# Local attention and the last tanh stage with one-pass products of split operands

## The chip, the cores and the metric

The kernel runs on one core of a Trainium2 chip. The metric is the device time of one execution in microseconds (us), the median of several runs. The core's engines are called by their short names: PE (TensorE, matrix products; PEld is its weight loading), DVE (VectorE), ACT (ScalarE), POOL (GpSimd) and SP, which issues DMAs. Each engine works through its own instructions in the order written, and waits on semaphores for the others.

## The reference

Eight sublayers follow each other on an input of 8 x 1024 x 256. Each adds its result to x. The two that the change touches are the first and the last:

```python
x = x + local_attention(layernorm(x), Wq, bq, Wk, bk, Wv, bv)   # the first
# q, k, v = xh @ W.T + b in groups of 64 tokens (1024 / 16 heads along the length)
# out = softmax(q @ k.T) @ v inside each group
...
x = x + tanh(((layernorm(x) @ weight) @ aux1) @ aux2 + bias)    # the last, and one more before
```

Everything is fp32. The other sublayers (two expert layers, a spectral attention, a second-order attention, the other tanh layer, a window attention) are as before.

## The kernel before, in words

x lies in on-chip memory (`R.X`) as 64 tiles of 128 tokens by 256 values. The stages run one after another, with a barrier between them.

**Local attention** (`local_attention`, tiles named `la_...`). Its loop runs over the 64 tiles, and on every engine an iteration i serves several tiles at different steps. The steps of one tile are:

- POOL: `normalize` (L2790) makes the normalised tile `xn`.
- PE: `turn_x` (L2574) transposes it in two pieces of 128 columns. ACT: `copy_xT` (L2654) copies the result to `xnT`.
- PE: `project` makes z = G x (L2585; G is the product of Wq and Wk, folded once at the start) and v (L2591; 273 columns, of which some are not v itself: one is a term that the scores need, eight feed the next stage's gate).
- DVE: `copy_z` (L2718) and `copy_v` (L2727) bring them from PSUM to SBUF. POOL: `add_row` makes `mask_row` (L2797) and `before` (L2798) from v.
- PE: `scores` (L2599). DVE: `mask_S` (L2735) adds `mask_row` and takes the maximum; it waits for `mask_ready`, that is, for the tile's `add_row`. ACT: `exponent` (L2660).
- PE: `turn_p` (L2606), ACT: `copy_pT` (L2667), PE: `weigh` (L2612; it waits for `x_ready` of the tile before).
- DVE: `residual` (L2740, L2744, L2746: reciprocal, gate part, X) and `next_stats` (L2751), the statistics for the next stage. In the first iterations DVE also takes the statistics of the tiles to come (L2687), 24 in iterations 0 to 4 and 32 in iterations 8 to 28.

The order on each engine is written by hand, in the loops at the end of each engine's block. The projection's results, the scores, the transposed probabilities and the output have one PSUM bank each, so the next tile's product waits until DVE or ACT has emptied it.

**Last tanh stage** (`tanh_ffn` with `out` given, tiles `t_...`). The three weights are folded into one matrix `wc` in an earlier stage. For each tile: PE transposes X (L196) four tiles ahead, ACT copies (L221), PE multiplies by `wc` (L204, two products of 256 columns), DVE scales and adds the bias (L246), ACT takes tanh (L227), POOL adds to X (L264), and SP sends eight tiles at a time to the output.

An fp32 product is two instructions on PE in the trace, each with its weight load. The type fp32r is taken in one instruction, with less precision. The expert stages before and after the change already use it: each operand is split into a high part (a copy to fp32r) and a low part (operand minus high), and the product is the sum of high x high, high x low and low x high.

The code with its line numbers:

## Time and profile before

| | |
|---|---|
| median of 3 runs | 3776.21 us (3773.47 to 3776.36) |
| profiled execution | 3772.48 us, of which span 3770.5 |
| PE busy | 3479.7 us, 92% |
| PEld busy | 3107.1 us, 82% |
| DVE busy | 2376.8 us, 63% |
| ACT busy | 2133.8 us, 57% |
| POOL busy | 1515.2 us, 40% |
| local attention | up to 232.9 us from the start, its loop from about 25 |
| last tanh stage | from 3690.5 to the end |

Busy shares are means over stages with different limits. The stage that the change touches most takes 5 to 6% of the span, so what happens there is read from its own stretch: a timeline of one tile, the waits of each engine, and the distance between two instructions of one kind. A line number names the line of the kernel that issued the instruction.

### The profile page before, as it was taken

Reading aid. Unit: us, or ns where it says so; the run is one execution under the profiler, and the core shown is the slowest. Engines: PE = TensorE matmul, PEld = TensorE weight load, DVE = VectorE, ACT = ScalarE, POOL = GpSimd, SP = SyncE. Lnnn points to the kernel's source line nnn. Section 1 sums busy time; section 2 is a strip of 40 time slices with the busy share of each in tenths; the row PEclk is TensorE's granted clock in tenths of the full one; section 3 lists DMA queues with packets and bytes.
Section 4 is the critical chain, followed back from the end, with each engine's and each line's share of the span. In section 5 each row is a group of like instructions: output and inputs, shape, how many; then the busy total and the mean of one; then the engine's idle time right before and its main releaser. Section 6 shows DMA issues by size and latency. Waiting matters only on the chain. (4 is left out here: it accounts for less than half of the span.)

```text
span 3770.5 us, 116189 instructions
## 1 busy us (share of the span) xinstructions
PE 3479.7 (92%) x44738; PEld 3107.1 (82%) x44738; DVE 2376.8 (63%) x6505; ACT 2133.8 (57%) x6562; POOL 1515.2 (40%) x2283
## 2 busy tenths in 40 slices
PE   8948999799849999799999999999988999999998
PEld 7838999677729999799898999989976877777777
DVE  6774555688765554455544444444446899999994
ACT  3345555455446555344444444444444888888895
POOL 3444665210035665344444444444446222222215
PEclk9979999899969999899999999999999999999999
DMA  3143443511153443300000000000000000000002
GB/s 123 39 144 99 93 92 60 146 47 52 50 186 92 93 93 71 101 3 3 3 3 3 3 3 3 3 3 3 3 6 16 2 2 2 2 2 2 2 2 94
DMA packets 137902, 164.64 MB, mean 44 GB/s; under 512 B 11392, under 2 KB 127264, under 8 KB 137376
## 3 DMA queue, kind: packets, MB, share of 16 engines
q1 hardware_dynamic: 112800, 123.81, 10.2%
q0 software_dynamic: 24576, 33.57, 5.3%
q8 instruction: 361, 5.91, 0.7%
q14 instruction: 165, 1.35, 0.1%
HBM read 97.18 MB, written 60.16 MB: 42 GB/s over the span
## 5 line engine op out<-in xcount | busy, mean ns | idle before, releaser
L2328 ACT ACTIVATE wa_S<-wa_S,wa_top 128x256 f32<-128x256 f32 x1024 | 512.5, 508 | 105.3 <-DVE wa_top L2396 104.3
L1912 DVE TENSOR_TENSOR so_raw<-so_rows,so_masks 128x1024 f32<-128x1024 f32 x256 | 313.5, 1225 | 227.4 <-PE so_rows L1612 219.8
L2396 DVE CUSTOM_DVE_ANT_0 wa_S<-wa_bank,wa_band 128x256 f32<-128x256 f32 x1024 | 366.8, 419 | 10.8 <-issue 10.1
L1991 POOL TENSOR_TENSOR so_more<-so_compact,so_head 128x384 f32<-128x384 f32 x224 | 185.4, 828 | 337.9 <-PE so_bankC L1694 307.9
L2245 PE MATMUL wa_bank<-ident,wa_S 128*128 128x128 f32 x2048 | 284.5, 277 | 29.3 <-ACT wa_probT L2335 28.7
L2245 PEld LDWEIGHTS wa_bank<-ident,wa_S 128*128 128x128 f32 x2048 | 229.8, 141 | 71.9 <-ACT wa_S L2328 35.7
L1901 DVE SCALAR_TENSOR_TENSOR so_compact<-so_compact,so_bankX 128x96 f32<-128x96 f32 x192 | 48.8, 254 | 356.1 <-PE so_bankX L1730 356.1
L1828 ACT COPY so_O<-so_bankC 128x128 f32<-128x128 f32 x256 | 68.4, 267 | 307.8 <-PE so_bankC L1694 307.8
L1996 POOL TENSOR_TENSOR so_OT<-so_O,so_OT 128x128 fp32r<-128x128 f32 x256 | 117.5, 459 | 307.8 <-ACT so_OT L1834 307.8
L626 POOL DMA_INDIRECT sum_dram<-y,rows x128 | 223.8, 1748 | 29.4 <-issue 27.1
L704 ACT ACTIVATE m4e_hT<-m_bank,m4e_bias 128x256 fp32r<-128x256 f32 x256 | 126.1, 493 | 151.4 <-PE m_bank L656 144.3
L704 ACT ACTIVATE m2e_hT<-m_bank,m2e_bias 128x256 fp32r<-128x256 f32 x256 | 126.3, 493 | 149.0 <-PE m_bank L656 141.3
L1641 PE MATMUL so_bankJ<-so_xnT,so_w 128*128 128x256 f32 x1500 | 208.0, 288 | 1.5 <-DVE so_xnT L1893 1.5
L2328 ACT ACTIVATION_READ_ACCUMULATOR wa_S<-wa_S,wa_top 128x1 f32 x1024 | 201.4, 197 | 0.0
L656 PE MATMUL m_bank<-m4e_exT,m_w_parts 128*128 128x256 f32 x1536 | 193.5, 285 | 0.7 <-issue 0.4
L656 PE MATMUL m_bank<-m2e_exT,m_w_parts 128*128 128x256 f32 x1536 | 193.2, 284 | 0.3 <-ACT m2e_h L704 0.3
L2404 DVE COPY wa_probT<-wa_bank 128x512 f32<-128x512 f32 x256 | 169.7, 689 | 31.4 <-PE wa_bank L2245 29.3
L656 PEld LDWEIGHTS m_bank<-m4e_exT,m_w_parts 128*128 128x128 f32 x1536 | 187.4, 189 | 1.1 <-issue 0.6
L656 PEld LDWEIGHTS m_bank<-m2e_exT,m_w_parts 128*128 128x128 f32 x1536 | 187.3, 189 | 0.6 <-ACT m2e_h L704 0.5
L1641 PEld LDWEIGHTS so_bankJ<-so_xnT,so_w 128*128 128x128 f32 x1500 | 185.3, 190 | 1.9 <-DVE so_xnT L1893 1.9
L670 PE MATMUL m_bank<-m_w_parts,m4e_hT 128*128 128x256 f32 x1536 | 186.2, 280 | 0.6 <-DVE m4e_pre L751 0.6
L670 PE MATMUL m_bank<-m_w_parts,m2e_hT 128*128 128x256 f32 x1536 | 186.1, 280 | 0.6 <-DVE m2e_pre L751 0.6
(451 smaller groups left out, 10065.9 us busy)
## 6 DMA issues: line engine op xcount, KB each, us to landing
m_w_raw<-in_L_ffn_W_dram SPq DMA_DIRECT2D x64, 512.0 KB, 3.8
sum_dram<-X SPq DMA_DIRECT2D x16, 1024.0 KB, 4.5
X<-sum_dram SPq DMA_DIRECT2D x16, 1024.0 KB, 7.7
X<-in_L_attn_a_x_dram SPq DMA_DIRECT2D x8, 1024.0 KB, 11.8
xn_dram<-m2r_xn SPq DMA_DIRECT2D x16, 512.0 KB, 4.5
sp_gx<-gate_dram SPq DMA_DIRECT2D x64, 128.0 KB, 2.7
xn_dram<-m4r_xn SPq DMA_DIRECT2D x16, 512.0 KB, 4.7
out_dram<-X SPq DMA_DIRECT2D x8, 1024.0 KB, 4.4
```

Source lines behind the costliest of these rows:

```text
L626: nc.gpsimd.indirect_dma_start(out=summed, out_offset=bass.IndirectOffsetOnAxis(ap=rows[:, s, u:u + 1], axis=0), in_=y[:, s % 2, u, :], in ...
L656: last = nc.tensor.matmul(bank[:, 0:2 * P], w_parts[:, par, a, c, f * P:(f + 1) * P], exT[:, s % 2, b, c], start=(n == 0), stop=(n == len( ...
L670: last = nc.tensor.matmul(by[u][:, 0:HID], hT[:, s % 2, a, f, u * P:(u + 1) * P], w_parts[:, par, b, 2 + f // QF, f % QF * HID:(f % QF + 1 ...
L704: last = nc.scalar.activation(to, bh[f % 4][:, 0:2 * P], ACT.Gelu_apprx_tanh, bias=bias[:, par, f:f + 1])
L1641: last = nc.tensor.matmul(bank[:, 2 * k * P:2 * (k + 1) * P], w[:, a, n, c, cols], xnT[:, b, c], start=(m == 0), stop=(m == 2 * len(PARTS) ...
L1912: nc.vector.tensor_tensor(AB[:, t % 2].rearrange("p h m t -> p h (m t)"), rows4[:, :, 0:2 * P], masks[:].rearrange("p m t -> p (m t)")[:, ...
L1991: nc.gpsimd.tensor_tensor(state[:, t % UT], compact[:, t % UT, :, None, :].broadcast_to([P, 3, HG, DK]), head[:, None, :, None].broadcast_ ...
L1996: nc.gpsimd.tensor_tensor(OT[:, 1, t % (2 * UT)], O[:, t % UT], OT[:, 0, t % (2 * UT)].bitcast(F32), ALU.subtract).then_inc(s_["O_ready"], 1)
L2245: last = nc.tensor.transpose(bT[q % 2][:, (2 * h + k) * P:(2 * h + k + 1) * P], S[:, n % 2, 2 * q + h, k * P:(k + 1) * P], R.ident[:])
L2328: nc.scalar.activation(S[:, n % 2, z], S[:, n % 2, z], ACT.Exp, bias=top[:, n % 2, z:z + 1], scale=-1.0, accum_out=sums[:, i % 2, SET * c ...
L2396: nc.vector.tensor_tensor_reduce(out=S[:, n % 2, z], in0=bS[g][:, eo * SPAN:(eo + 1) * SPAN], in1=band[:], scale=-(D ** -0.5), scalar=3e38 ...
L2404: nc.vector.tensor_copy(probT[:, n % 2, 2 * q:2 * q + 2].rearrange("p h k t -> p (h k t)"), bT[q % 2][:]).then_inc(s_["T_dve"], 1)
```

## The change

In local attention the folded product z and the value product v become products of split fp32r operands, three in place of one: for each of G, the value weights `wv` and the transposed x there is a high and a low part. Transposes, the copy of them and z are now done for pairs of tiles (p is the pair's number: tiles 2p and 2p+1), with 256 columns a product; v, with one column added to make its width even, stays per tile. ACT now copies the transposed pair twice (the high part and the fp32 value, 512 columns each), and POOL subtracts them for the low part (`low_xT`). The low parts of the weights are made once by DVE. All steps behind the projection come one iteration later, and each engine's loop has a new order. In the last tanh stage alone (`split`) the product becomes six fp32r products in place of two fp32 ones; ACT's copy is the high part, and DVE makes the low part of each tile.

```diff
@@ -162,9 +162,13 @@
-        wc = sb("wc", [P, HC, HID])
+        split = out is not None
+        PARTS = ((0, 0), (0, 1), (1, 0)) if split else ((0, 0),)
+        KIND = F32R if split else F32
+        wc = sb("wc", [P, 2 if split else 1, HC, HID], KIND)
+        wc_raw = sb("wc_raw", [P, HC, HID]) if split else wc[:, 0]
-        xT = sb("xT", [P, RING, HC, P])
+        xT = sb("xT", [P, RING, 2 if split else 1, HC, P], KIND)
...
-                    for c in range(HC):
-                        last = nc.tensor.matmul(psY[i % len(psY)][:, 0:HID], xT[:, i % RING, c, :], wc[:, c, :], start=(c == 0), stop=(c == HC - 1))
+                    steps = [(a, b, c) for a, b in PARTS for c in range(HC)]
+                    for n, (a, b, c) in enumerate(steps):
+                        last = nc.tensor.matmul(psY[i % len(psY)][:, 0:HID], xT[:, i % RING, a, c, :], wc[:, b, c, :],
+                                                start=(n == 0), stop=(n == len(steps) - 1))
                     last.then_inc(psY_ready, 1)
...
-                pe.wait_ge(wc_loaded, 16)
+                if split:
+                    pe.wait_ge(wc_ready, 1)
+                else:
+                    pe.wait_ge(wc_loaded, 16)
...
-                    nc.scalar.copy(xT[:, i % RING].rearrange("p c t -> p (c t)"), psT[i % len(psT)][:, 0:HID]).then_inc(xT_ready, 1)
+                    nc.scalar.copy(xT[:, i % RING, 0].rearrange("p c t -> p (c t)"), psT[i % len(psT)][:, 0:HID]
+                                   ).then_inc(xT_high if split else xT_ready, 1)
...
                 std_of_var(nc, act, R, var_ready, std_ready)
+                if split:
+                    act.wait_ge(wc_loaded, 16)
+                    nc.scalar.copy(wc[:, 0], wc_raw[:]).then_inc(wc_high, 1)
...
+                def low_xT(i):
+                    dve.wait_ge(xT_high, i + 1)
+                    high, low = (xT[:, i % RING, part].rearrange("p c t -> p (c t)") for part in range(2))
+                    nc.vector.tensor_tensor(low, psT[i % len(psT)][:, 0:HID], high.bitcast(F32), ALU.subtract).then_inc(xT_ready, 1)
+
...
+                if split:
+                    dve.wait_ge(wc_high, 1)
+                    nc.vector.tensor_tensor(wc[:, 1], wc_raw[:], wc[:, 0].bitcast(F32), ALU.subtract).then_inc(wc_ready, 1)
+                    for i in range(AHEAD):
+                        low_xT(i)
                 for i in range(NT + 4):
                     if i < NT:
                         add_bias(i)
+                    if split and i + AHEAD < NT:
+                        low_xT(i + AHEAD)
...
@@ -2461,6 +2487,9 @@
+    EVEN = WIDE + 1
+    PARTS = ((0, 0), (0, 1), (1, 0))
+    RING = 3
...
-        G = sb("G", [P, HC, HID])
-        wv = sb("wv", [P, HC, WIDE])
+        G = sb("G", [P, 2, HC, HID], F32R)
+        wv, wv_parts = sb("wv", [P, HC, EVEN]), sb("wv_parts", [P, 2, HC, EVEN], F32R)
...
-        xnT = sb("xnT", [P, 4, HC, P])
-        zT = sb("zT", [P, 2, HC, P])
+        xnT, xnT_parts = sb("xnT", [P, RING, HC, 2 * P]), sb("xnT_parts", [P, RING, 2, HC, 2 * P], F32R)
+        zT = sb("zT", [P, 2, HC, 2 * P])
...
-                def turn_x(i):
-                    pe.wait_ge(xn_ready, i + 1)
-                    if i >= 1:
-                        pe.wait_ge(xT_ready, i)
+                def turn_x(p):
+                    pe.wait_ge(xn_ready, 2 * p + 2)
+                    if p >= 1:
+                        pe.wait_ge(xT_ready, p)
                     for c in range(HC):
-                        last = nc.tensor.transpose(ps_xT[:, c * P:(c + 1) * P], xn[:, i % 4, c * P:(c + 1) * P], R.ident[:])
+                        for j in range(2):
+                            last = nc.tensor.transpose(ps_xT[:, (2 * c + j) * P:(2 * c + j + 1) * P], xn[:, (2 * p + j) % 4, c * P:(c + 1) * P], R.ident[:])
                     last.then_inc(xT_done, 1)
 
-                def project(i):
-                    pe.wait_ge(xT_ready, i + 1)
+                def project_z(p):
+                    pe.wait_ge(xT_low, p + 1)
+                    if p == 0:
+                        pe.wait_ge(w_split, 1)
+                    if p >= 1:
+                        pe.wait_ge(z_ready, p)
+                    for e in range(HC):
+                        for n, (a, b, c) in enumerate((a, b, c) for a, b in PARTS for c in range(HC)):
+                            last = nc.tensor.matmul(ps_z[:, e * 2 * P:(e + 1) * 2 * P], G[:, a, c, e * P:(e + 1) * P], xnT_parts[:, p % RING, b, c],
+                                                    start=(n == 0), stop=(n == HC * len(PARTS) - 1))
+                    last.then_inc(z_done, 1)
+
+                def project_v(i):
                     if i == 0:
                         pe.wait_ge(w_ready, 8)
-                    if i >= 1:
-                        pe.wait_ge(z_ready, i)
-                    for e in range(HC):
-                        for c in range(HC):
-                            last = nc.tensor.matmul(ps_z[:, e * P:(e + 1) * P], G[:, c, e * P:(e + 1) * P], xnT[:, i % 4, c],
-                                                    start=(c == 0), stop=(c == HC - 1))
-                    last.then_inc(z_done, 1)
+                        pe.wait_ge(w_split, 2)
                     if i >= 1:
                         pe.wait_ge(v_ready, i)
-                    for c in range(HC):
-                        last = nc.tensor.matmul(ps_v[:, 0:WIDE], xnT[:, i % 4, c], wv[:, c, :], start=(c == 0), stop=(c == HC - 1))
+                    for n, (a, b, c) in enumerate((a, b, c) for a, b in PARTS for c in range(HC)):
+                        last = nc.tensor.matmul(ps_v[:, 0:EVEN], xnT_parts[:, i // 2 % RING, a, c, own_half(i)], wv_parts[:, b, c],
+                                                start=(n == 0), stop=(n == HC * len(PARTS) - 1))
                     last.then_inc(v_done, 1)
...
-                        last = nc.tensor.matmul(ps_S[:, 0, :], zT[:, i % 2, e, :], xnT[:, i % 4, e], start=(e == 0), stop=(e == HC - 1))
+                        last = nc.tensor.matmul(ps_S[:, 0, :], zT[:, i // 2 % 2, e, own_half(i)], xnT[:, i // 2 % RING, e, own_half(i)],
+                                                start=(e == 0), stop=(e == HC - 1))
...
-                for i in range(NT + 5):
-                    if 5 <= i:
-                        weigh(i - 5)
-                    if 4 <= i < NT + 4:
-                        turn_p(i - 4)
+                for i in range(NT + 6):
+                    if 6 <= i:
+                        weigh(i - 6)
+                    if 5 <= i < NT + 5:
+                        turn_p(i - 5)
+                    if 3 <= i < NT + 3:
+                        scores(i - 3)
+                    if i % 2 == 0 and i < NT:
+                        turn_x(i // 2)
+                    if i % 2 == 0 and 2 <= i < NT + 2:
+                        project_z(i // 2 - 1)
                     if 2 <= i < NT + 2:
-                        scores(i - 2)
-                    if i < NT:
-                        turn_x(i)
-                    if 1 <= i < NT + 1:
-                        project(i - 1)
+                        project_v(i - 2)
...
-                nc.scalar.copy(G[:].rearrange("p c d -> p (c d)"), ps_z[:]).then_inc(w_ready, 1)
+                nc.scalar.copy(G[:, 0].rearrange("p c d -> p (c d)"), ps_z[:]).then_inc(w_ready, 1)
...
-                def copy_xT(i):
-                    act.wait_ge(xT_done, i + 1)
-                    if i >= 4:
-                        act.wait_ge(v_done, i - 3)
-                        act.wait_ge(S_done, i - 3)
-                    nc.scalar.copy(xnT[:, i % 4].rearrange("p c t -> p (c t)"), ps_xT[:, 0:HID]).then_inc(xT_ready, 1)
+                def copy_xT(p):
+                    act.wait_ge(xT_done, p + 1)
+                    if p >= RING:
+                        act.wait_ge(v_done, 2 * (p - RING) + 2)
+                        act.wait_ge(S_done, 2 * (p - RING) + 2)
+                    nc.scalar.copy(xnT_parts[:, p % RING, 0].rearrange("p c t -> p (c t)"), ps_xT[:])
+                    nc.scalar.copy(xnT[:, p % RING].rearrange("p c t -> p (c t)"), ps_xT[:]).then_inc(xT_ready, 1)
...
+                for i in range(NT + 5):
+                    if 5 <= i:
+                        copy_pT(i - 5)
+                    if i % 2 == 0 and i < NT:
+                        copy_xT(i // 2)
+                    if 3 <= i < NT + 3:
+                        exponent(i - 3)
...
+                dve.wait_ge(w_ready, 1)
+                nc.vector.tensor_tensor(G[:, 1].rearrange("p c d -> p (c d)"), ps_z[:], G[:, 0].rearrange("p c d -> p (c d)").bitcast(F32), ALU.subtract
+                                        ).then_inc(w_split, 1)
...
+                c.then(nc.vector.tensor_copy(wv_parts[:, 0], wv[:]))
+                nc.vector.tensor_tensor(wv_parts[:, 1], wv[:], wv_parts[:, 0].bitcast(F32), ALU.subtract).then_inc(w_split, 1)
+
+                def copy_z(p):
+                    dve.wait_ge(z_done, p + 1)
+                    if p >= 2:
+                        dve.wait_ge(S_done, 2 * p - 2)
+                    nc.vector.tensor_tensor(zT[:, p % 2], ps_z[:].rearrange("p (e t) -> p e t", e=HC),
+                                            bz[:, :, None].broadcast_to([P, HC, 2 * P]), ALU.add).then_inc(z_ready, 1)
...
-                for i in range(NT + 7):
-                    if 5 <= i < NT + 5:
-                        residual(i - 5)
+                for i in range(NT + 8):
+                    if 6 <= i < NT + 6:
+                        residual(i - 6)
+                    if 3 <= i < NT + 3:
+                        mask_S(i - 3)
+                    if i % 2 == 0 and 2 <= i < NT + 2:
+                        copy_z(i // 2 - 1)
                     if 2 <= i < NT + 2:
-                        mask_S(i - 2)
-                    if 1 <= i < NT + 1:
-                        copy_z(i - 1)
-                        copy_v(i - 1)
+                        copy_v(i - 2)
-                        begin, end = GROUPS[g - 1][0], a - 4
+                        begin, end = GROUPS[g - 1][0], a - 5
...
+                    if i >= 8:
+                        next_stats(i - 8)
...
+                nc.gpsimd.memset(wv[:, :, WIDE:EVEN], 0.0)
...
                     if i >= 4:
-                        pool.wait_ge(xT_done, i - 3)
+                        pool.wait_ge(xT_done, (i - 4) // 2 + 1)
                     nc.gpsimd.tensor_scalar(xn[:, i % 4], R.X[:, i, :], R.rstd[:, i:i + 1], R.shift[:, i:i + 1],
                                             ALU.mult, ALU.add).then_inc(xn_ready, 1)
+
+                def low_xT(p):
+                    pool.wait_ge(xT_ready, p + 1)
+                    nc.gpsimd.tensor_tensor(xnT_parts[:, p % RING, 1], xnT[:, p % RING], xnT_parts[:, p % RING, 0].bitcast(F32), ALU.subtract
+                                            ).then_inc(xT_low, 1)
...
-                for i in range(NT + 2):
-                    if i < NT:
-                        normalize(i)
-                    if 2 <= i:
-                        add_row(i - 2)
+                normalize(0)
+                normalize(1)
+                for i in range(NT + 3):
+                    if i % 2 == 0 and i < NT:
+                        low_xT(i // 2)
+                    if 3 <= i:
+                        add_row(i - 3)
+                    if i + 2 < NT:
+                        normalize(i + 2)
```

What POOL does in two tiles in the middle of local attention, before: `mask_row` and `before` are `add_row`, `xn` is `normalize`.

```order
L2797 TENSOR_SCALAR la_mask_row<-la_mask,la_v 128x128 [waits la_masked,la_v_ready]
L2798 TENSOR_SCALAR la_before<-la_v,var 128x8
L2790 TENSOR_SCALAR la_xn<-X,rstd,shift 128x256 [waits la_xT_done,la_scaled]
L2797 TENSOR_SCALAR la_mask_row<-la_mask,la_v 128x128 [waits la_masked,la_v_ready]
L2798 TENSOR_SCALAR la_before<-la_v,var 128x8
L2790 TENSOR_SCALAR la_xn<-X,rstd,shift 128x256 [waits la_xT_done,la_scaled]
```

And now, the same place, beginning with an even iteration; `la_xnT_parts` is the low part of a pair:

```order
L2846 TENSOR_TENSOR la_xnT_parts<-la_xnT,la_xnT_parts 128x512 [waits la_xT_ready]
L2853 TENSOR_SCALAR la_mask_row<-la_mask,la_v 128x128 [waits la_masked,la_v_ready]
L2854 TENSOR_SCALAR la_before<-la_v,var 128x8
L2841 TENSOR_SCALAR la_xn<-X,rstd,shift 128x256 [waits la_xT_done,la_scaled]
L2853 TENSOR_SCALAR la_mask_row<-la_mask,la_v 128x128 [waits la_masked,la_v_ready]
L2854 TENSOR_SCALAR la_before<-la_v,var 128x8
L2841 TENSOR_SCALAR la_xn<-X,rstd,shift 128x256 [waits la_xT_done,la_scaled]
```

The instruction for pair p stands ahead of `mask_row` of tile 2p - 3 and waits for ACT's copies of pair p.

PE in the same place, now, from the even iteration's `scores` (tile 2p - 3) to the next but one iteration's `weigh`:

```order
L2639 MATMUL la_ps_S<-la_xnT,la_zT 128x128 [waits la_masked,la_z_ready]
L2639 MATMUL la_ps_S<-la_xnT,la_zT 128x128
L2608 MATMUL la_ps_xT<-ident,la_xn 128x128 [waits la_xT_ready,la_xn_ready]
L2608 MATMUL la_ps_xT<-ident,la_xn 128x128 x3
L2619 MATMUL la_ps_z<-la_xnT_parts,la_G 128x256 [waits la_z_ready,la_xT_low]
L2619 MATMUL la_ps_z<-la_xnT_parts,la_G 128x256 x11
L2630 MATMUL la_ps_v<-la_wv_parts,la_xnT_parts 128x274 [waits la_v_ready]
L2630 MATMUL la_ps_v<-la_wv_parts,la_xnT_parts 128x274 x5
L2653 MATMUL la_ps_o<-la_v,la_probT 128x264 [waits la_x_ready,la_pT_ready]
L2647 MATMUL la_ps_pT<-ident,la_S 128x128 [waits la_pT_ready,la_prob_ready]
L2639 MATMUL la_ps_S<-la_xnT,la_zT 128x128 [waits la_masked,la_z_ready]
```

Pair p is transposed only behind the scores of tile 2p - 3, and the product that follows it is that of the pair before.

DVE in an even iteration, now, and the start of the odd one:

```order
L2783 MEMSET turnstile 1x1 [waits la_pT_done,la_mask_ready,la_S_done]
L2784 ISA la_S,la_top<-la_ps_S,la_mask_row 128x128
L2784 ISA la_top 128x1
L2767 TENSOR_TENSOR la_zT<-la_ps_z,la_bz 128x512 [waits la_S_done,la_z_done]
L2776 TENSOR_TENSOR la_v<-la_ps_v,la_bv_all 128x273 [waits la_mask_ready,la_before_ready,la_o_done,la_v_done]
L2800 BN_STATS raw<-X 128x6 [waits la_x_ready]
L2789 RECIPROCAL la_share<-la_total 128x1 [waits la_prob_ready]
L2793 SCALAR_TENSOR_TENSOR L<-la_ps_o,la_share,la_before 128x8 [waits la_before_ready,la_share_ready,la_o_done]
L2795 SCALAR_TENSOR_TENSOR X<-la_ps_o,la_share,X 128x256
```

`mask_S` (the first three rows) stands ahead of `copy_z` for a pair, which was there for every tile before and is now in every other iteration.

## Rows read from the trace of the kernel before

**Rows 1.** Table by stretch (length, busy us of each engine, TensorE clock, DMA), local attention.

```profile
140.00:200.00 60.00, 60.00 (x418) 54.58 (x417) 41.48 (x179) 20.71 (x80) 28.75 (x60) 1.00 0.14 48
```

**Rows 2.** Timeline (start, us, engine, line, operation), one tile of local attention.

```profile
123.25 0.28 DVE L2735 CUSTOM_DVE_ANT_0 la_S<-la_ps_S,la_mask_row 128x128 f32<-128x128 f32 x1
...
123.46 0.42 DVE L2718 TENSOR_TENSOR la_zT<-la_ps_z,la_bz 128x256 f32<-128x256 f32 x1
...
124.11 0.61 PE L2612 MATMUL la_ps_o<-la_v,la_probT 128*128 128x264 f32 x2
124.31 0.44 DVE L2727 TENSOR_TENSOR la_v<-la_ps_v,la_bv_all 128x273 f32<-128x273 f32 x1 [0.43 <-PE la_ps_v L2591]
...
124.66 0.42 DVE L2751 BATCH_NORM_STATS2 raw<-X 128x6 f32<-128x256 f32 x1
124.84 0.61 POOL L2797 TENSOR_SCALAR la_mask_row<-la_mask,la_v 128x128 f32<-128x128 f32 x1 [1.60 <-DVE la_v L2727]
...
125.00 0.15 DVE L2740 RECIPROCAL la_share<-la_total 128x1 f32<-128x1 f32 x1
125.11 0.38 PE L2574 MATMUL la_ps_xT<-ident,la_xn 128*128 128x128 f32 x2
...
125.23 0.23 DVE L2744 SCALAR_TENSOR_TENSOR L<-la_ps_o,la_share,la_before 128x8 f32<-128x8 f32 x1
125.32 1.06 PE L2585 MATMUL la_ps_z<-la_xnT,la_G 128*128 128x128 f32 x8
125.38 0.48 DVE L2746 SCALAR_TENSOR_TENSOR X<-la_ps_o,la_share,X 128x256 f32<-128x256 f32 x1
...
125.52 0.37 ACT L2654 COPY la_xnT<-la_ps_xT 128x256 f32<-128x256 f32 x1 [1.45 <-PE la_ps_xT L2574]
...
126.22 1.09 PE L2591 MATMUL la_ps_v<-la_wv,la_xnT 128*128 128x273 f32 x4
...
127.14 0.61 PE L2612 MATMUL la_ps_o<-la_v,la_probT 128*128 128x264 f32 x2
```

**Rows 3.** Timeline, end of the loop: `weigh` waits for the residual.

```profile
227.11 0.47 DVE L2746 SCALAR_TENSOR_TENSOR X<-la_ps_o,la_share,X 128x256 f32<-128x256 f32 x1
...
227.73 0.68 PE L2612 MATMUL la_ps_o<-la_v,la_probT 128*128 128x264 f32 x2 [0.69 <-DVE X L2746]
```

**Rows 4.** Timeline, window attention: two copies of a transposed pair, POOL's low part.

```profile
2930.18 0.57 ACT L2315 CAST wa_xnT<-wa_bank 128x512 fp32r<-128x512 f32 x1
...
2931.31 1.29 POOL L2120 TENSOR_TENSOR wa_xnT<-y,wa_xnT 128x512 fp32r<-128x512 f32 x1 [4.82 <-ACT y L2318]
...
2932.55 1.05 POOL L2133 TENSOR_TENSOR wa_QM<-wa_Q,wa_pick 128x512 f32<-128x512 f32 x1
```

**Rows 5.** Timeline, window attention: two DVE instructions of 512 columns from PSUM.

```profile
3683.61 1.29 DVE L2404 COPY wa_probT<-wa_bank 128x512 f32<-128x512 f32 x2 [2.87 <-PE wa_bank L2245]
```

**Rows 6.** Timeline, expert stage: fp32r products of 256 columns.

```profile
1312.16 6.00 PE L656 MATMUL m_bank<-m4e_exT,m_w_parts 128*128 128x256 f32 x48
```

**Rows 7.** Timeline: `mask_S` of tiles 5, 25 and 59, and the next stage.

```profile
48.54 0.29 DVE L2735 CUSTOM_DVE_ANT_0 la_S<-la_ps_S,la_mask_row 128x128 f32<-128x128 f32 x1
...
109.43 0.28 DVE L2735 CUSTOM_DVE_ANT_0 la_S<-la_ps_S,la_mask_row 128x128 f32<-128x128 f32 x1
...
213.84 0.28 DVE L2735 CUSTOM_DVE_ANT_0 la_S<-la_ps_S,la_mask_row 128x128 f32<-128x128 f32 x1
...
232.92 0.30 SPq L342 DMA_DIRECT2D m2r_wg_rows<-in_L_ffn_Wg_dram  x1
```

**Rows 8.** Timeline, last tanh stage: two tiles' products.

```profile
3753.78 1.03 PE L204 MATMUL t_psY<-t_wc,t_xT 128*128 128x256 f32 x4
...
3754.86 1.03 PE L204 MATMUL t_psY<-t_wc,t_xT 128*128 128x256 f32 x4
```

**Rows 9.** Table by stretch, PE alone, spectral attention: clock with gaps.

```profile
1016.00:1020.00 4.00, 3.12 (x80) 1.00 0.01 2
...
1032.00:1036.00 4.00, 2.58 (x8) 0.82 0.14 39
```

More of the change, by code:

```diff
@@ L177, in tanh_ffn @@
         pre_ready, th_ready, x_ready = sem("pre_ready"), sem("th_ready"), sem("x_ready")
+        wc_high, wc_ready, xT_high = sem("wc_high"), sem("wc_ready"), sem("xT_high")
         with nc.Block() as block:
@@ L181, in _ @@
             def _(sp):
-                sp.dma_start(wc[:], R.centred_dram).then_inc(wc_loaded, 16)
+                sp.dma_start(wc_raw[:] if split else wc_raw, R.centred_dram).then_inc(wc_loaded, 16)
                 sp.dma_start(bias_all[:], bias.rearrange("(a d) -> a d", a=1).broadcast_to([P, HID])).then_inc(bias_loaded, 16)
@@ L2506, in local_attention, with own_half @@
         ones_ready, cleared, wg_ready = sem("ones_ready"), sem("cleared"), sem("wg_ready")
+        w_split, xT_low = sem("w_split"), sem("xT_low")
         before_ready, centre_ready, L_ready, x_out = sem("before_ready"), sem("centre_ready"), sem("L_ready"), R.x_out
+        def own_half(j):
+            return slice(j % 2 * P, (j % 2 + 1) * P)
         source = A["L0_attn_a_x"]
@@ L2592, in project @@
                     last.then_inc(v_done, 1)
                 def scores(i):
-                    pe.wait_ge(z_ready, i + 1)
+                    pe.wait_ge(z_ready, i // 2 + 1)
                     if i >= 1:
@@ L2667, in copy_pT @@
                     nc.scalar.copy(probT[:, i % 4], ps_pT[:, 0]).then_inc(pT_ready, 1)
-                for i in range(NT + 4):
-                    if i < NT:
-                        copy_xT(i)
-                    if 4 <= i < NT + 4:
-                        copy_pT(i - 4)
-                    if 2 <= i < NT + 2:
-                        exponent(i - 2)
+                for i in range(NT + 5):
[5 more added lines that the diff above has]
+                        exponent(i - 3)
                     for g in (1, 2):
-                        if i == GROUPS[g][0] - 3:
+                        if i == GROUPS[g][0] - 4:
                             deviations(g)
@@ L2711, in _ @@
                 dve.wait_ge(loaded, 9 * 16)
+                dve.wait_ge(w_ready, 1)
+                nc.vector.tensor_tensor(G[:, 1].rearrange("p c d -> p (c d)"), ps_z[:], G[:, 0].rearrange("p c d -> p (c d)").bitcast(F32), ALU.subtract
+                                        ).then_inc(w_split, 1)
                 dve.wait_ge(w_ready, 8)
-                def copy_z(i):
-                    dve.wait_ge(z_done, i + 1)
-                    if i >= 2:
-                        dve.wait_ge(S_done, i - 1)
-                    nc.vector.tensor_tensor(zT[:, i % 2], ps_z[:, 0:HID].rearrange("p (e t) -> p e t", e=HC),
-                                            bz[:, :, None].broadcast_to([P, HC, P]), ALU.add).then_inc(z_ready, 1)
+                c.then(nc.vector.tensor_copy(wv_parts[:, 0], wv[:]))
[6 more added lines that the diff above has]
+                                            bz[:, :, None].broadcast_to([P, HC, 2 * P]), ALU.add).then_inc(z_ready, 1)
                 def copy_v(i):
@@ L2773, in _ @@
                             scales(g)
-                    if i >= 7:
-                        next_stats(i - 7)
+                    if i >= 8:
+                        next_stats(i - 8)
                 dve.wait_ge(L_ready, NT)
@@ L2805, in centres @@
                                             wg_sum[:, None, :].broadcast_to([P, b - a, E]), ALU.mult).then_inc(centre_ready, 1)
-                for i in range(NT + 2):
-                    if i < NT:
-                        normalize(i)
-                    if 2 <= i:
-                        add_row(i - 2)
+                normalize(0)
[7 more added lines that the diff above has]
+                        normalize(i + 2)
                     for g, (a, b) in enumerate(GROUPS):
```

## The prediction

> **What bounds the kernel now.** I read the stretch table of local attention first, then the timeline of one tile, then the distance between instructions of one kind. In the table the reader is to see PE busy for all 60.00 of 60 us at full clock, with DVE at 41.48 and POOL at 28.75 [rows 1]. The timeline shows the same from inside: PE's rows follow each other without a gap, one tile takes 127.14 - 124.11 = 3.03 us, z takes 0.90 of it (125.32 to 126.22) and v 0.92 (126.22 to 127.14), while ACT, DVE and POOL wait for PE: POOL's `mask_row` stood idle for 1.60 us before v came [rows 2]. So this stage is bound by PE, and fewer PE cycles are worth something as long as nobody else becomes last. In the last tanh stage a tile takes 3754.86 - 3753.78 = 1.08 us on PE [rows 8].
>
> **The change on PE.** An fp32r product of 256 columns costs 6.00 / 48 = 0.125 us in the expert stage [rows 6]. For a pair of tiles PE then has 12 of these for z (1.50), 12 of 274 columns for v (0.80 a tile, 1.60), four transposes (twice 0.21, from 125.11 to 125.32: 0.42), and twice `weigh`, `turn_p` and `scores` (1.00 each, 124.11 to 125.11) [rows 2]: 5.52 us, against 6.06 before. If PE stayed last, 32 pairs would give 17 us.
>
> **What becomes last instead.** I follow the waits in the new order. In an even iteration 2p POOL has to do the low part of pair p before `mask_row` of tile 2p - 3. The low part waits for ACT's two copies, these for PE's transposes of pair p, and the transposes stand on PE behind the scores of that same tile 2p - 3. So the scores are done and `mask_S` can't take them: it waits for a mask row that is queued behind a pair that has only just been transposed. On DVE, behind `mask_S`, stand `copy_z` of the pair before (needed by the next scores), `copy_v`, a statistic, and the residual of the odd iteration; PE's `weigh` of the next even iteration waits for that residual, and behind `weigh` stand the scores and the transposes of pair p + 1. That closes a ring, once per pair. Its links, start to start:
> - transposes to ACT: 0.41 for two (125.11 to 125.52), two more 0.21: 0.62 [rows 2]
> - ACT's first copy to POOL's low part: 2931.31 - 2930.18 = 1.13, the same three instructions in the window attention; low part to POOL's next: 1.24 [rows 4]
> - `mask_row` 0.61 and a hand-over of 0.09 (as 124.31 + 0.44 to 124.84): 0.70; `mask_S` to `copy_z` 0.21 [rows 2]
> - `copy_z`, now 512 columns: 1.29 / 2 = 0.64 [rows 5]
> - `copy_v` to statistic 0.35, to reciprocal 0.34, to L 0.23, to X 0.15 [rows 2]; X to `weigh` 227.73 - 227.11 = 0.62 [rows 3]; `weigh` to transposes 1.00 [rows 2]
>
> The sum is 7.23 us a pair. PE works 5.52 of it. In iterations 8 to 27 DVE also takes 32 statistics ahead, 1.6 per iteration at 0.34; those of the even iteration lie in the ring: 7.77.
>
> Before, a pair took (213.84 - 109.43) / 17 = 6.14 in the late part (`mask_S` of tiles 25 and 59) and (109.43 - 48.54) / 10 = 6.09 in the early part (tiles 5 and 25) [rows 7].
> - Late: 17 pairs x (7.23 - 6.14) = +18.5
> - Early: 10 pairs x (7.77 - 6.09) = +16.8
> - Start, up to `mask_S` of tile 5: the first pair needs two normalised tiles, two more transposes, 0.76 more of ACT (1.13 less 0.37) and the low part of 1.24 before any product; the mask row of tile 1 then goes once round 0.62 + 1.13 + 1.24 + 0.70 = 3.7; DVE's splits of the weights (three instructions of 512 and 548 columns, about 1.8) hide partly in these waits. I take +7, an estimate, with 3 (fill alone) and 11 (nothing hidden) as bounds.
> - End, from `mask_S` of tile 59: no transposes come any more, the ring is open, and two pairs run at PE's pace of about 5.1 rather than 6.1: -2
> - Sum for local attention: +40.3
>
> Costed at nothing: ACT's second copy and POOL's longer work as such (both are far from full, 20.71 and 28.75 of 60 [rows 1]; they cost only as links), the smaller number of `copy_z` instructions, the memsets. The odd iterations' `mask_row` waits for `copy_v` and is ready 0.3 us before DVE comes to it; if it were late, that much is added.
>
> The Trainium skill ("GPSIMD Engine Reference", "Performance versus the Vector engine") gives about 2.6 cycles an element for a two-input operation on GpSimd; an estimate from it for 512 elements at 1.2 GHz is 1.11 us, where the trace has 1.29 for this very operation [rows 4]. By the page the ring would be about 0.15 shorter and the whole 4 us less; the row is used. The same page's engine table says to leave elementwise work on two inputs to VectorE, which speaks against this change: here the operation sits in the ring.
>
> **The last tanh stage.** Six products at 0.125 and 0.21 of transposes: 0.96 against 1.08 a tile, -0.12 x 64 = -7.7. DVE gets one more instruction of 256 columns per tile; two of about 0.45 (0.42 for `copy_z`, 0.48 for X [rows 2]) are under 0.96, so PE stays last. The split of `wc` on ACT and DVE delays the first product by about 1.3 and cheaper products at the start give back half: +0.7. Sum -7. The bounds are -13 (a product at 256 columns / 2.4 GHz = 0.107) and 0.
>
> **Sum.** +40.3 - 7 = +33.3. Against the profiled execution of 3772.5 that is 3805.8; the median of the runs shown lies 3.7 above that execution, so 3809.5, I say 3809.
>
> **Rivals.**
> - *PE stays last, faster.* The mask row is never behind the low part in time, so the ring is not there. Then DVE is just longer than PE between the even v and the next `weigh` (0.20 + 0.35 + 0.34 + 0.23 + 0.15 + 0.62 = 1.89, then 1.00 + 0.42 + 1.50 + 0.80): 5.61 late, 6.15 early. 17 x -0.53 + 10 x 0.06 + 3 at the start - 2 at the end - 7 = -14: 3762. For it speaks PE's lead in the rows of before and POOL's idle 1.60 [rows 2]; against it that the transposes come behind the scores on PE itself, so the low part can't be early. It decides as soon as a pair takes less than 6.2.
> - *The clock falls in the new gaps.* PE would stand idle some 1.7 us per pair in two pieces. In the spectral attention the clock held 1.00 through 3.12 busy of 4 us, and fell to 0.82 in a stretch with 2.58 busy in few long pieces [rows 9]. The new share, 5.52 / 7.23 = 76%, is like the first (78%). If it fell to the lower level throughout, the ring's PE links (1.42) double: 27 x 1.42 = +38, 3848.
> - *The tanh stage gains nothing*, since DVE and ACT have a chain of their own with the low part between copy and bias: 3816.
> - *The product's price is too low.* In the ring PE isn't last, so this costs almost nothing there.
>
> **Chances.** The ring as described, with or without the tanh gain: 0.84 (0.09 of it without). Clock falls: 0.07. PE stays last: 0.09. The range of the likeliest alone takes the start (-4 to +4), the ring's links (each hand-over unsure by 0.03, some 0.3 a pair, 27 pairs: 8) and the tanh stage (-6 to +7): 3794 to 3824. Taking in some of the clock's case and of a looser ring gives 3785 to 3831. 0.2% is 7.5 us, about what a measurement of this kernel can tell from no change. Faster than that 0.08, within it 0.05, slower 0.87.
>
> **What the profile would show.** Right: in local attention `mask_S` in even iterations waits for POOL's `mask_row`, about 2.5 us after PE finished the scores; POOL's low part waits for ACT; PE's `scores` of the odd iteration wait for `copy_z` (a gap of 1.3 to 1.7 us); `mask_S` of every second tile is 7.2 apart late and 7.8 early; the next stage starts near 273 rather than 232.9; the clock stays 1.00. In the tanh stage two tiles' products are 0.96 apart. Wrong: a pair under 6.2, or PE without gaps; a clock of 0.5 in the middle of the stage; a tanh stage at 1.08.

## The result, and the profile after

The changed kernel takes 3826.77 us (median of 4 runs, 3823.51 to 3827.69) against 3775.80 for the kernel before in the same job: 1.0133 times as long, with a 95% interval of 1.012 to 1.0146. That is slower, as forecast. The time lies inside the forecast range and 18 us above the forecast 3809. One execution of stats_odd, an experiment below, took 5905.67 us at a mean granted clock of 0.655; its figures go by the other three.

First the table by stretch of the changed kernel (columns as in [rows 1]). 140 to 200 answers to [rows 1].

```profile
30.00:80.00 50.00, 38.39 (x239) 34.34 (x240) 29.14 (x114) 17.66 (x47) 25.57 (x44) 0.88 0.05 17
80.00:140.00 60.00, 46.77 (x293) 41.43 (x291) 33.15 (x136) 16.87 (x54) 28.76 (x49) 0.89 0.11 36
140.00:200.00 60.00, 47.77 (x329) 42.30 (x330) 33.48 (x146) 22.42 (x67) 32.43 (x56) 0.97 0.11 36
200.00:250.00 50.00, 40.55 (x292) 36.02 (x291) 25.90 (x114) 16.71 (x53) 27.43 (x46) 1.00 0.13 43
```

PE was busy in 60.00 of 60 us and is now busy in 47.77; no other engine is near full. When no engine is full, read the chain of waits. The second thing to see is the clock column: 0.88 and 0.89 up to 140, 0.97 after it and 1.00 only at the end.

The timeline of one pair in the late part, changed kernel (start, duration, engine, line, operation, idle before and its releaser), answers to [rows 2] and [rows 4]:

```profile
201.76 0.61 PE L2639 MATMUL la_ps_S<-la_xnT,la_zT 128*128 128x128 f32 x4
...
202.20 0.60 PE L2608 MATMUL la_ps_xT<-ident,la_xn 128*128 128x128 f32 x4
...
202.84 0.59 ACT L2697 CAST la_xnT_parts<-la_ps_xT 128x512 fp32r<-128x512 f32 x1 [0.62 <-PE la_ps_xT L2608]
...
204.00 1.28 POOL L2846 TENSOR_TENSOR la_xnT_parts<-la_xnT,la_xnT_parts 128x512 fp32r<-128x512 f32 x1 [2.59 <-ACT la_xnT L2698]
...
205.25 0.61 POOL L2853 TENSOR_SCALAR la_mask_row<-la_mask,la_v 128x128 f32<-128x128 f32 x1
...
205.97 0.06 DVE L2783 MEMSET turnstile<- 1x1 f32 x1 [3.32 <-issue]
206.03 0.29 DVE L2784 CUSTOM_DVE_ANT_0 la_S<-la_ps_S,la_mask_row 128x128 f32<-128x128 f32 x1
...
206.24 0.69 DVE L2767 TENSOR_TENSOR la_zT<-la_ps_z,la_bz 128x512 f32<-128x512 f32 x1
...
206.84 0.43 DVE L2776 TENSOR_TENSOR la_v<-la_ps_v,la_bv_all 128x273 f32<-128x273 f32 x1
...
206.98 0.71 PE L2639 MATMUL la_ps_S<-la_xnT,la_zT 128*128 128x128 f32 x4 [1.43 <-DVE la_zT L2767]
207.19 0.42 DVE L2800 BATCH_NORM_STATS2 raw<-X 128x6 f32<-128x256 f32 x1
...
207.91 0.47 DVE L2795 SCALAR_TENSOR_TENSOR X<-la_ps_o,la_share,X 128x256 f32<-128x256 f32 x1
...
208.53 0.68 PE L2653 MATMUL la_ps_o<-la_v,la_probT 128*128 128x264 f32 x2
...
209.60 0.27 PE L2608 MATMUL la_ps_xT<-ident,la_xn 128*128 128x128 f32 x1
```

This is the ring of the prediction, link by link: transposes to ACT 0.64, to the low part 1.16, to `mask_row` 1.25, to `mask_S` 0.78, to `copy_z` 0.21, to `copy_v` 0.60, to the statistic 0.35, to X 0.72, to `weigh` 0.62, and 1.07 from there to the next transposes (209.60): 7.40. DVE's wait of 3.32 us ahead of the memset of `mask_S` is named "issue" in the row. It is POOL's mask row all the same: that starts at 205.25, takes 0.61, and the memset comes 0.11 after its end. PE finished the scores of this tile long before (201.76 + 0.61), 3.7 us ahead of `mask_S`.

Answering to [rows 7], the timeline of the changed kernel at `mask_S` of tiles 5, 25 and 59, then the next stage:

```profile
59.31 0.29 DVE L2784 CUSTOM_DVE_ANT_0 la_S<-la_ps_S,la_mask_row 128x128 f32<-128x128 f32 x1
...
146.65 0.29 DVE L2784 CUSTOM_DVE_ANT_0 la_S<-la_ps_S,la_mask_row 128x128 f32<-128x128 f32 x1
...
273.00 0.29 DVE L2784 CUSTOM_DVE_ANT_0 la_S<-la_ps_S,la_mask_row 128x128 f32<-128x128 f32 x1
...
288.58 0.30 SPq L368 DMA_DIRECT2D m2r_wg_rows<-in_L_ffn_Wg_dram  x1
```

Term by term, all measured against [rows 7]:

| part of local attention | forecast | measured |
|---|---|---|
| start, to tile 5 | +7 | +10.8 (59.31 - 48.54) |
| early, 10 pairs | +16.8 | +26.4 (87.34 - 60.89) |
| late, 17 pairs | +18.5 | +21.9 (126.35 - 104.41) |
| end | -2 | -3.5 (15.58 - 19.08) |
| sum | +40.3 | +55.7 (288.58 - 232.92) |

Seventeen late pairs took 7.43 on average. The ten early ones were uneven: 9.01, 7.72, 9.32, 8.06, 9.53, 7.73, 9.18, 8.05, 9.50, 9.24. The stretch table of single windows of the changed kernel shows why:

```profile
62.00:66.00 4.00, 3.86 (x17) 3.58 (x18) 2.23 (x9) 1.64 (x5) 0.09 (x1) 0.57 0.01 4
63.00:65.50 2.50, 2.50 (x13) 2.50 (x12) 1.23 (x5) 0.65 (x2) 0.00 (x0) 0.50 0.02 7
65.50:78.00 12.50, 9.58 (x70) 8.51 (x69) 6.89 (x28) 3.82 (x13) 7.93 (x14) 0.99 0.00 1
80.50:83.00 2.50, 2.50 (x14) 2.50 (x14) 0.55 (x2) 1.06 (x3) 0.00 (x0) 0.53 1.02 344
83.00:95.50 12.50, 9.24 (x68) 8.17 (x67) 7.01 (x28) 3.37 (x12) 7.56 (x13) 1.00 0.01 3
```

In each of the six pairs above 9 the granted clock fell to 0.5, the lower level (1.2 GHz), for 3.4 us (0.57 over the 4 us of the first row: half of 3.4 us is lost), just where `weigh`, `turn_p`, the scores and the transposes run one after the other. Each fall began within 0.5 us of the start of `weigh`. The transfers that fill the fourth row (344 GB/s) aren't what goes with it: the first fall has next to none. The timeline of PE of the changed kernel, the same four steps in a short pair and in a long one:

```profile
71.15 0.69 PE L2653 MATMUL la_ps_o<-la_v,la_probT 128*128 128x264 f32 x2 [0.40 <-DVE X L2795]
71.67 0.27 PE L2647 MATMUL la_ps_pT<-ident,la_S 128*128 128x128 f32 x1
71.78 0.61 PE L2639 MATMUL la_ps_S<-la_xnT,la_zT 128*128 128x128 f32 x4
72.22 0.60 PE L2608 MATMUL la_ps_xT<-ident,la_xn 128*128 128x128 f32 x4
```

```profile
79.20 1.01 PE L2653 MATMUL la_ps_o<-la_v,la_probT 128*128 128x264 f32 x2 [0.72 <-DVE X L2795]
80.00 0.42 PE L2647 MATMUL la_ps_pT<-ident,la_S 128*128 128x128 f32 x1
80.22 1.06 PE L2639 MATMUL la_ps_S<-la_xnT,la_zT 128*128 128x128 f32 x4
81.07 1.06 PE L2608 MATMUL la_ps_xT<-ident,la_xn 128*128 128x128 f32 x4
```

The last tanh stage, answering to [rows 8] (products of two tiles, changed kernel):

```profile
3780.51 0.96 PE L210 MATMUL t_psY<-t_wc,t_xT 128*128 128x256 f32 x6
...
3781.45 0.96 PE L210 MATMUL t_psY<-t_wc,t_xT 128*128 128x256 f32 x6
```

A tile takes 0.94 instead of 1.08. From the start of the last tanh stage to the end of the span it is 72.97 instead of 79.95 us: -7.0, as forecast. The stages between, whose code is the same, took 6.5 longer; that is dealt with below.

### The profile page after: what moved, and what is told of

It is laid out like the page before. It is cut to its first block and busy times, and to the rows that moved or that the text cites. A ratio compares the mean times of both kernels' runs of the same rounds, so it can differ in the third digit from the quotient of the medians.

```text
span 3825.7 us, 116394 instructions
## 1 busy us (share of the span) xinstructions
PE 3473.5 (91%) x44866; PEld 3106.5 (81%) x44866; DVE 2394.5 (63%) x6541; ACT 2148.3 (56%) x6563; POOL 1554.2 (41%) x2316
## 5 line engine op out<-in xcount | busy, mean ns | idle before, releaser
L652 POOL DMA_INDIRECT sum_dram<-y,rows x128 | 221.7, 1732 | 29.4 <-issue 27.1
```

Source lines behind the costliest of these rows:

```text
L652: nc.gpsimd.indirect_dma_start(out=summed, out_offset=bass.IndirectOffsetOnAxis(ap=rows[:, s, u:u + 1], axis=0), in_=y[:, s % 2, u, :], in ...
```

## The experiments

Each ratio is to the kernel before in the same job; times are medians. "Pairs" are mean distances of `mask_S` of tiles 5 to 25 (early) and 25 to 59 (late) in the trace. "Next stage" is its start in the trace, counted from the start of the kernel; it takes in when POOL normalises its first tile, at 24.6 to 25.8 in eight traces and some 3 us later, at 27.6 and 27.8, in row_first and la_only, whose code up to there is that of the changed kernel.

| kernel | us | ratio, 95% interval | early pair | late pair | next stage |
|---|---|---|---|---|---|
| before | 3776.8 | | 6.09 | 6.14 | 232.9 |
| changed | 3826.8 | 1.012 to 1.0146 | 8.73 | 7.43 | 288.6 |
| row_first | 3771.4 | 0.9975 to 0.9993 | 6.34 | 5.54 | 231.9 |
| tanh_only | 3771.0 | 0.9972 to 0.9991 | 6.09 | 6.14 | 233.3 |
| la_only | 3834.7 | 1.0137 to 1.0168 | 8.19 | 7.43 | 286.3 |
| stats_odd | 3821.4 | 1.0095 to 1.0132 | 7.47 | 7.49 | 277.2 |
| low_twice | 3898.8 | 1.0305 to 1.0336 | 10.29 | 10.23 | 360.1 |
| z_one_pass | 3835.7 | 1.0139 to 1.017 | 8.78 | 7.90 | 297.5 |
| pe_filled | 3816.2 | 1.0089 to 1.012 | 7.93 | 7.43 | 280.7 |
| best | 3763.3 | 0.9951 to 0.9978 | 5.75 | 5.55 | 221.7 |

**row_first: the ring opened by exchanging two steps on POOL**

```diff
-                    if i % 2 == 0 and i < NT:
-                        low_xT(i // 2)
                     if 3 <= i:
                         add_row(i - 3)
+                    if i % 2 == 0 and i < NT:
+                        low_xT(i // 2)
```

> Only the order on POOL in even iterations is changed: the mask row of tile 2p-3 first, then the low part of pair p. If the ring through POOL's low part is what costs (my theory), mask_S no longer waits for it: pairs of local attention fall from 7.4 (late) and 8.7 (early) to 5.6 and 6.1 us, the clock stays at its upper level, the next stage starts near 230 us, and the whole is near 3767 us, a little faster than the kernel before. If the added work itself is what costs (second copy, low part, products with 256 columns, whatever the order), pairs stay above 7 and the whole above 3815.

Measured 3771.38. Not one instruction is added or removed, and 55 us are gone. The stretch table of row_first:

```profile
140.00:200.00 60.00, 59.68 (x450) 55.54 (x449) 43.00 (x181) 27.12 (x87) 44.12 (x76) 1.00 0.16 54
```

PE is full again, with a late pair of 5.54 where the prediction put PE's work at 5.52. So the order on POOL is the cause of the loss, and in the late part the products are worth what they were meant to be worth, 0.60 a pair. Over the whole of local attention that isn't much: the early pairs are longer than before (6.34 against 6.09), the start too, and from the first normalised tile to the next stage it takes 204.3 us (27.6 to 231.9) against 208.1 (24.8 to 232.9). Most of the 5.4 us by which row_first beats the kernel before can come from the last tanh stage.

**tanh_only and la_only: one half of the change each.** tanh_only has the local attention of before with the new `tanh_ffn`; la_only is the changed kernel with:

```diff
-        split = out is not None
+        split = False
```

> Local attention as before, the last tanh stage with split operands. Theory: the stage is shorter by 7 us (0.93 against 1.08 us a tile, a later start given back partly), so 3769 us. Rival: the gain is an accident of the profiled run and the later start of the stage eats it, 3776 us.

> Local attention as changed, the last tanh stage as before. Theory: 56 us longer in local attention, nothing else, so 3832 to 3834 us, 7 above the changed kernel. Rival: the two parts hang together by the clock or by the transfers at the end, and the sum of the two single changes is not the whole.

Measured 3771.03 and 3834.66. The tanh stage alone is worth -5.8 in the medians (3771.03 against 3776.78), and leaving it out of the changed kernel costs +7.9. la_only's late pairs are those of the changed kernel to the hundredth (7.43). Its early pairs are 7.7 to 8.1 where the clock is 1.00 and 9.3 to 9.5 in the two in which it fell, at 120 and 130 us. So the same instructions give different numbers of falls in different executions.

**stats_odd: the statistics made ahead taken out of the ring**

```diff
                             upto = (b - a) * (i - begin + 1) // (end - begin + 1)
+                            if g == 2 and i % 2 == 0:
+                                upto = ahead[g]
```

> The changed kernel, but the 32 statistics that DVE takes ahead in iterations 8 to 27 are all taken in odd iterations, where they don't lie in the ring. Theory: the early pairs take 7.4 us as the late ones do and the clock no longer falls there, since a ring of 7.4 keeps it up in the late part: 87 - 74 = 13 us less, 3814 us. Rival A: the clock falls in the early part for another reason (its position in time), then only the 0.55 us of statistics a pair go, pairs of 8.2, 3821 us. Rival B: DVE is full in odd iterations and the time stays, 3827 us.

Measured 3821.37. In the trace the theory's mechanism holds: nine of the ten early pairs are 7.40 to 7.42, the length of the late ring, the granted clock is 1.00 through all of them (one fall comes behind, at 135 us, in a first late pair of 8.53), and the next stage starts 11.4 us earlier. The median fell by only 5.4. The rest isn't found again in local attention but in the stages behind it, which took longer in this trace (below). By the time alone this experiment would have pointed to the rival.

**low_twice: POOL makes the low part twice**

```diff
+                                            ).then_inc(low_once, 1)
+                    pool.wait_ge(low_once, p + 1)
+                    nc.gpsimd.tensor_tensor(xnT_parts[:, p % RING, 1], xnT[:, p % RING], xnT_parts[:, p % RING, 0].bitcast(F32), ALU.subtract
```

> Changed kernel in which POOL makes each pair's low part twice (1.27 us more per pair on POOL, whose busy share is 41%). Theory of the ring (low part, then mask row, mask_S, copy_z, residual, transposes, low part): each of 27 to 31 pairs grows by 1.27 + about 0.06 of wait: 7.40 -> 8.7 late, and the time by 36 to 41 to 3863 to 3868. Rival (POOL's low part has slack, the pair is set by TensorE or by copy_z alone): within 3 of 3827. If the clock also falls because TensorE idles longer in each pair, up to 1.4 more per late pair: up to 3890.

Measured 3898.83: 72 more, twice what the low part alone explains and a little beyond what I allowed for. The timeline of low_twice shows both halves in one pair:

```profile
244.29 1.06 PE L2639 MATMUL la_ps_S<-la_xnT,la_zT 128*128 128x128 f32 x4
...
245.15 1.06 PE L2608 MATMUL la_ps_xT<-ident,la_xn 128*128 128x128 f32 x4
...
246.24 0.59 ACT L2697 CAST la_xnT_parts<-la_ps_xT 128x512 fp32r<-128x512 f32 x1 [1.44 <-PE la_ps_xT L2608]
...
247.40 1.29 POOL L2846 TENSOR_TENSOR la_xnT_parts<-la_xnT,la_xnT_parts 128x512 fp32r<-128x512 f32 x1 [4.05 <-ACT la_xnT L2698]
...
248.77 1.26 POOL L2849 TENSOR_TENSOR la_xnT_parts<-la_xnT,la_xnT_parts 128x512 fp32r<-128x512 f32 x1
...
250.01 0.61 POOL L2856 TENSOR_SCALAR la_mask_row<-la_mask,la_v 128x128 f32<-128x128 f32 x1
```

The second low part adds 248.77 - 247.40 = 1.37 to the ring. The other 1.4 of a pair of 10.21 against 7.40 is the clock, which now falls in every late pair: the scores take 1.06 instead of 0.61, the transposes 1.06 instead of 0.60, and transposes to ACT 1.09 instead of 0.64. A POOL that is busy 41% of the time is on the path with the whole of this instruction, and lengthening it makes PE's own links dearer.

**z_one_pass: z from the high parts alone** (8 of 12 products of a pair left out, so z is less precise)

```diff
-                        for n, (a, b, c) in enumerate((a, b, c) for a, b in PARTS for c in range(HC)):
+                        for c in range(HC):
```

> Changed kernel whose folded product z is made from the high parts alone (8 of 12 products of a pair left out, so z is less precise); every copy, subtraction and wait stays. 8 x 0.122 = 0.98 us less of TensorE per pair. Theory of the ring: z is made an iteration before it is asked for, TensorE isn't last, no change: 3824 to 3829, late pairs 7.40. Rival 1 (TensorE is last): pairs 0.98 shorter, 3827 - 27 = 3800. Rival 2 (the clock falls when TensorE has less to do): the ring's TensorE links (1.42) double in some or all pairs, late pairs 7.4 to 8.8, 3835 to 3865.

Measured 3835.67: with 0.98 of PE's 5.52 us per pair taken away the kernel is 9 us slower. Ten of its late pairs are 7.38 to 7.39 and seven, the first among them, 7.55 to 9.2. The stretch table of z_one_pass:

```profile
140.00:200.00 60.00, 42.94 (x262) 36.99 (x262) 31.59 (x137) 21.79 (x64) 30.35 (x51) 0.91 0.11 36
```

The clock is 0.91 here against 0.97 in the changed kernel. That settles that PE's work isn't what a pair waits for. The late part of this trace has six falls of the clock, where those of the changed kernel, la_only and pe_filled have none and that of stats_odd has one; so less work on PE went with more falls. That is one trace, but all four runs (3833.74 to 3838.03) are longer than the longest of the changed kernel (3827.69).

**pe_filled: products added into PE's gap**

```diff
+                    if 9 <= i < 32 and i % 2 == 1:
+                        for n in range(6):
+                            nc.tensor.matmul(ps_idle[:, 0:2 * P], G[:, 0, 0, 0:P], wv_parts[:, 0, 0, 0:2 * P], start=True, stop=True)
```

> Changed kernel with six more fp32r products of 256 columns (0.73 us) on TensorE ahead of the scores of iterations 9, 11 .. 31, into a bank that nothing reads: there it waits 1.3 to 1.7 us for copy_z. Theory: the granted clock of 0.5 in about half of the early pairs is what makes these 9.0 to 9.5 instead of 7.7 to 8.05, and it comes from TensorE's idle share; with the gap filled the early pairs are 7.7 to 8.05 all through (clock 1.00 between 60 and 147), -3 to -8: 3819 to 3824. Rival: the clock falls for another reason or by chance: the dips stay, 3827, or the added products delay the scores: 3830 to 3835.

Measured 3816.15, 10.6 less than the changed kernel, beyond the 3 to 8 that I expected. The stretch table of pe_filled:

```profile
80.00:140.00 60.00, 49.96 (x363) 45.04 (x363) 37.95 (x157) 19.12 (x60) 31.97 (x54) 1.00 0.08 27
```

The clock is 1.00 in every window from 58 to 148, and all ten early pairs are 7.72 to 8.06. Work that nobody needs, 0.73 us a pair, made the kernel faster: the early part became 8.1 us shorter (10 x (8.73 - 7.93)). So that is the clock's share of the early loss. The number of falls varies between executions by itself (la_only), so one trace alone wouldn't do; but all four runs of pe_filled (3813.36 to 3819.52) are shorter than the shortest of the changed kernel (3823.51). The next stage starts 7.9 us earlier; what the median gains beyond that lies in stages whose code is the same.

**best: the ring opened, and the rest put into DVE's wait for z.** row_first, and:

```diff
+                    if GROUPS[1][0] <= i <= GROUPS[2][0] - 5 and i % 2 == 0:
+                        upto = ahead_by(2, i + 1)
+                        for k in range(ahead[2], upto):
+                            stats(GROUPS[2][0] + k)
+                        ahead[2] = upto
                     if i % 2 == 0 and 2 <= i < NT + 2:
                         copy_z(i // 2 - 1)
...
-                normalize(0)
-                normalize(1)
+                for i in range(4):
+                    normalize(i)
...
-                    if i + 2 < NT:
+                    if 4 <= i + 2 < NT:
```

(`ahead_by` is the old rule for how many are due.)

> Changed kernel with three moves: POOL adds the mask rows of a tile ahead of the low part of a pair; at the start it normalizes tiles 2 and 3 ahead of the first low part; the statistics made ahead for the third group stand on DVE ahead of copy_z in even iterations, where DVE waits for z anyway. From the traces of row_first (early pairs 6.33, late 5.54, row order alone, 3771.4 median): if TensorE is last throughout, the early pairs fall to 5.6 to 5.8 (10 x -0.6 = -6) and the start by 1.9 (the second pair's transposes no longer wait for tile 3 behind the low part): 3771.4 - 8 = about 3763, la end near 225 in the trace. Rival: the statistics held up copy_z and with it the scores, pairs stay at 6.3: 3769 to 3773.

Measured 3763.33, 0.9964 times the kernel before [0.9951 to 0.9978]: the version that beats both. The next stage starts at 221.7, 11 us ahead of before. The stretch table of best, and what DVE waits for in its late part, 150 to 200 (us in total, times, longest):

```profile
60.00:140.00 80.00, 79.95 (x600) 74.16 (x599) 68.69 (x276) 37.37 (x116) 60.26 (x102) 1.00 0.16 54
140.00:200.00 60.00, 59.68 (x450) 55.46 (x449) 43.27 (x185) 26.70 (x86) 43.80 (x76) 1.00 0.11 37
```

```profile
DVE la_zT L2767 <- PE la_ps_z L2619: 11.7, 9, 1.4
```

PE is full from 60 to the end of the loop, and DVE waits for z rather than the reverse. Of the 8 us against row_first the early pairs make 5.9 (10 x (6.34 - 5.75)), and the start 2.2: from the first normalised tile to the first mask it takes 11.1 instead of 13.3.

## Why the prediction was right, and where it was short

**Direction and mechanism: right, and shown.** PE was last before and is not in the changed kernel. The ring closes through POOL's order, and opening it there gives the 55 us back. Two of the prediction's own signs came out otherwise: the next stage starts at 288.6 rather than near 273, and the clock was at 0.5 in the middle of the stage, which was named as a sign of being wrong. The wait of `mask_S` behind the end of the scores, given as about 2.5 us, is 3.7; the prediction's own links from the transposes to `mask_S` add up to 3.69.

**The ring: 7.40 rather than 7.23.** The links from the rows of before were each within 0.08. The two largest misses are hand-overs: `mask_row` to `mask_S` 0.78 for 0.70, `weigh` to transposes 1.07 for 1.00. 17 late pairs make +2.9 of it, and single pairs of 7.57 and 7.75 the rest of the +3.4.

**The early part: +26.4 rather than +16.8.** Without falls of the clock an early pair is 7.93 (pe_filled), 0.16 above the forecast, the same miss as in the late ring: 1.6. The falls are 8.1 more. This is the step that failed. I gave the clock's rival a chance of 0.07 because PE's share of 76% was close to that of a stretch that had held its clock [rows 9], and thought of it as all or nothing. Its price per pair was right: 1.42 forecast, 1.2 to 1.5 measured in single pairs against the same pairs of pe_filled. What was wrong is the either-or, and with it the clock's term in the sum, which stood at nothing: the clock fell in six of the ten early pairs and in none of the late ones, whose ring is without the statistics made ahead.

**The start: +10.8 rather than +7.** The first mask comes 5.1 later (37.99 against 32.89), and tiles 0 to 5 take 5.7 more (21.32 against 15.65), since they already run in the ring: row_first, without it, takes 16.35. Its clock also falls once between tiles 0 and 5, as that of the changed kernel does (45.3 to 48.7), so the fall alone doesn't make the 5.7. One piece was missed: on PE the transposes of pair 1 stand ahead of z of pair 0 and waited for tile 3, which POOL normalised behind the low part. In best, where tiles 2 and 3 come first, it takes 11.1 from the first normalised tile to the first mask, instead of 13.1 (12.7 to 13.5 in the four other traces with that start and the same products). What the clock adds here no run separates: at the start it is at 0.5 for 13.7 us in the changed kernel and for 10.2 before.

**The end: -3.5 rather than -2.** Same sign, small.

**The tanh stage: -7.0, as forecast**, and tanh_only and la_only show it apart from the rest.

**Costed at nothing: 6.5 us in the stages between.** Their code is unchanged. From the first normalised tile of the next stage to the last transposed probabilities of the window attention the trace of before takes 3447.6 us, and the nine other traces 3450.2 to 3459.2, tanh_only among them with 3454.5, whose local attention is that of before. It doesn't follow the change in local attention. Part of it is which execution was profiled: before's, at 3772.48, is shorter than every other of its runs (median 3775.80), and the changed kernel's, at 3827.69, is the longest of its four (median 3826.77). In medians the two kernels are 51.0 apart, and local attention and the tanh stage explain 48.7 of it. Why the stages differ from execution to execution is open; no run here tests it. A term of some 5 us for stages that one doesn't touch belongs in a range.

**How near the number came.** Against the profiled execution the forecast was 3805.8 and the trace shows 3827.7: 21.9 too little, of which 15.4 are local attention and 6.5 the stages between. The forecast of the median had 3.7 on top, for the distance of before's median from its trace, while the changed kernel's median lies 0.9 below its trace; that made 17.3 of the 21.9, and is luck. The measured time lies outside the range of the likeliest case alone (3794 to 3824) and inside the stated one, which had been widened for the clock and a looser ring. The lower bound of the tanh stage works out at -14 (64 x (0.64 + 0.21 - 1.08) + 0.7) rather than -13; nothing hangs on it.

**The two rivals that lost.** "PE stays last" was priced at 3762 with 5.61 and 6.15 per pair. That is row_first, nearly to the number (5.54 and 6.34), which took the mechanism out and kept the rest. Its time of 3771.4 is 9 above that price: the price had 3 for the start, and `mask_S` of tile 5 came 8.7 later (57.23 against 48.54), 2.8 of it because the first tile was normalised later in this trace. "The product's price is too low" was said to cost nothing in the ring; z_one_pass shows that TensorE's time has no direct weight there.

## What to carry to other kernels

When a step is batched for pairs, look on each in-order engine at what now stands behind the batched instruction, and whether what releases it depends on that. A single exchange of two POOL steps was worth 55 us, and no busy share showed it. First order the ready small step ahead of the large waiting one; then put spare work into the wait that is left. Once PE is no longer full, price its links at the lower clock too, pair by pair and not for the whole stage.

## What the hardware did that I had not expected

Taking work off TensorE made the kernel slower (z_one_pass, +8.9 us), and giving it useless work made it faster (pe_filled, -10.6). The falls of the granted clock to 0.5 are short, 3.4 us each. In the changed kernel they came in six of ten early pairs, together with `weigh` behind the shorter of the pair's two gaps (0.4 to 0.7 us; the longer, 1.4 us, is ahead of the odd iteration's scores), and lay on four short steps that stand in the ring, so that each cost 1.2 to 1.5 us. The same instructions took a different number of them in two executions (la_only: 1.00 from 52 to 120, falls in two pairs after that).
